# Turning the combined expert rows: from TensorE transposes to an HBM round trip with VectorE block transposes, and a new order of scores and projection

## The reference

```
xn  = layernorm(x)
q, k, v = xn @ w_qkv.T + b_qkv
s   = softmax(q k^T / sqrt(512)) v @ w_out.T + b_out
full_w = softmax of the two largest router logits, zero for the other 6 experts
combined = sum_e full_w[e] * silu(xn @ expert_w[e] + expert_b[e])
y   = xn + combined @ proj_w + proj_b
g   = silu(norm_w * y / rms(y))
out = x + s * g
```

## Time and profile before

| | |
|---|---|
| time, median of 3 runs (lowest to highest) | 490.71 us (489.35 to 492.29) |
| the profiled execution: its own time | 490.71 us |
| its span, first to last instruction | 489.0 us |
| busy: TensorE, VectorE, ScalarE, GpSimd | 98%, 64%, 42%, 42% of the span |
| TensorE's granted clock, mean | 0.999 of 2.4 GHz |

### The profile page before, as it was taken

The page is one execution under the profiler, slowest core; times in us unless marked ns, Lnnn a source line. Parts: engine busy times, 40 slices in busy tenths (PEclk is TensorE's granted clock), DMA queues, the critical chain, the costliest instruction groups (busy, mean ns, idle before and its releaser), DMA issues.

```text
span 489.0 us, 7145 instructions
## 1 busy us (share of the span) xinstructions
PE 478.2 (98%) x2146; PEld 388.1 (79%) x2147; DVE 312.5 (64%) x474; ACT 207.7 (42%) x300; POOL 205.4 (42%) x289
## 2 busy tenths in 40 slices
PE   6999999999999999999999999999999999999995
PEld 3688787888888888878888888878888878888884
DVE  2657152578632436979888888762597754857762
ACT  1265463143331154736444444322655441644550
POOL 2145210005887859703000000744568873377234
PEclk9999999999999999999999999999999999999999
DMA  8764999966888599897996666897555864445512
GB/s 309 272 238 166 379 382 369 390 207 227 294 294 304 188 334 304 252 295 205 262 282 202 195 200 184 310 305 267 158 156 170 264 192 147 138 158 170 172 47 84
DMA packets 77630, 115.77 MB, mean 237 GB/s; under 512 B 6608, under 2 KB 36320, under 8 KB 77600
## 3 DMA queue, kind: packets, MB, share of 16 engines
q1 hardware_dynamic: 63872, 77.62, 50.4%
q0 software_dynamic: 7440, 25.45, 14.7%
q10 hardware_dynamic: 6288, 12.33, 7.1%
HBM read 66.09 MB, written 49.28 MB: 236 GB/s over the span
## 4 chain that ended last, share of the span: by engine, by line
PE 92%; DVE 3%; DMA 2%; issue 2%; SPq 0%; ACT 0%; DVEq 0%
PE ab L1589 20%; PE ab L1590 20%; PE ab L1591 20%; PE sc L1589 7%; PE sc L1591 7%; PE sc L1590 7%; PE sc L1605 3%; PE tp L1595 2%; DMA xg<-rows_scratch 2%; PE tp L1639 2%; DVE y L1468 1%; PE sc L1668 1%; DMA raw_v<-in_w_qkv 1%; PE ab L1613 1%; PE sc L1671 1%
## 5 line engine op out<-in xcount | busy, mean ns | idle before, releaser
L781 POOL DMA_INDIRECT y<-y_scratch,pos x32 | 33.3, 1042 | 88.8 <-DMA y_scratch<-yt_so 74.2
L1589 PE MATMUL ab<-W,st_h 128*128 x156 | 60.8, 390 | 0.6 <-DVE st_l L1297 0.6
L1591 PE MATMUL ab<-W,st_l 128*128 x156 | 60.7, 389 | 0.0
L1590 PE MATMUL ab<-W,st_h 128*128 x156 | 60.7, 389 | 0.0
L764 POOL DMA_INDIRECT rows_scratch<-xb,pos x32 | 31.2, 974 | 51.0 <-DVEq L1285 42.8
L1589 PE MATMUL sc<-xt_h,t_h 128*128 128x512 f32 x128 | 50.1, 391 | 0.0
L1591 PE MATMUL sc<-xt_h,t_l 128*128 128x512 f32 x128 | 49.8, 389 | 0.0
L1590 PE MATMUL sc<-xt_l,t_h 128*128 128x512 f32 x128 | 49.8, 389 | 0.0
L1026 ACT CAST st_h<-tp 128x512 fp32r<-128x512 f32 x39 | 22.9, 587 | 41.1 <-PE ab L1591 39.0
L1353 DVE TENSOR_REDUCE small<-sc 128x1 f32<-128x1024 f32 x16 | 19.5, 1222 | 24.3 <-PE sc L1591 21.9
L1589 PEld LDWEIGHTS ab<-W,st_h 128*128 128x128 f32 x156 | 29.3, 188 | 7.1 <-issue 1.0
(11 more groups left out here) (270 smaller groups left out, 1197.2 us busy)
## 6 DMA issues: line engine op xcount, KB each, us to landing
rows_scratch<-xn ACTq DMA_DIRECT2D x3, 3328.0 KB, 20.2
xb<-in_expert_w POOLq DMA_DIRECT2D x6, 1024.0 KB
xn<-rows_scratch SPq DMA_DIRECT2D x48, 128.0 KB, 3.4
xg<-rows_scratch SPq DMA_DIRECT2D x44, 128.0 KB
y_scratch<-yt_own SPq DMA_DIRECT2D x20, 256.0 KB, 3.1
y_scratch<-yt_so SPq DMA_DIRECT2D x19, 256.0 KB, 2.9
p_scratch<-prob SPq DMA_DIRECT2D x9, 512.0 KB, 2.9
rows_scratch<-xs SPq DMA_DIRECT2D x16, 256.0 KB, 5.9
```

The lines of the kernel that those rows point to most:

```text
L781: pool.indirect_dma_start(y[:, q, :], None, y_d, bass.IndirectOffsetOnAxis(pos[:, GB * s + p:GB * s + p + 1], 0))\
L1589: nc.tensor.matmul(dst, lh, rh, start=start, stop=False)
L1590: nc.tensor.matmul(dst, lh, rl, start=False, stop=False)
L1591: return nc.tensor.matmul(dst, ll, rh, start=False, stop=stop)
```

## The change

The combined rows are no longer transposed by TensorE. ScalarE's queue sends the two tiles of `y1` to HBM (`send_combined`, one transfer), waits for it and fetches them back into `y2` in four transfers of 32 partitions each, in pieces of 128 channels (`fetch_combined`); VectorE turns them with two block transposes (`c_turn`). `y2` is read back in another order of channels, so `add_bias` in the expert stage now writes its rows with the blocks of 32 channels permuted. The semaphore `tp_full` is left to the last probabilities; `p1_turned` counts both kinds of turn by the new table `TURN`, and GpSimd's gathers wait on it. In each step of the loop TensorE does `scores` before `project`. On VectorE `row_max` moves ahead of `add_product`; on ScalarE `exp` moves ahead of `squares`, with a send ahead of `gate` and a fetch behind `exp`. `bc_done` is merged into `pre`.

```diff
+    c_d = nc.dram_tensor("c_scratch", (GB, 2, P, D), F32).ap()
+    c_v = c_d.rearrange("p t s h -> p s t h")
+    c_q = c_d.rearrange("p t (r s) (a f) -> p a s t r f", r=4, a=4)
...
-              + [u for j in range(GB) for u in ([("p", j + 2, 0), ("p", j + 2, 1)] if j + 2 < GB else [])
-                 + ([("t", 1, 1, n) for n in range(KC)] if j == QB - 2 else []) + [("a", 1, j)]]):
+              + [u for j in range(GB) for u in ([("t", 1, 1, n) for n in range(KC)] if j == QB - 2 else [])
+                 + ([("p", j + 2, 0), ("p", j + 2, 1)] if j + 2 < GB else []) + [("a", 1, j)]]):
...
-                    pool.wait_ge(tp_full, j + 3)
+                    pool.wait_ge(p1_turned, TURN["c", j + 2])
...
+            def send_combined(p):
+                act.wait_ge(c_done, 2 * p + 2)
+                act.dma_start(c_v[p], y1[:, 2 * (p % 2):2 * (p % 2) + 2, :]).then_inc(comb_out, 16)
+
+            def fetch_combined(p):
+                act.wait_ge(comb_out, 16 * (p + 1))
+                for a in range(4):
+                    act.dma_start(y2[32 * a:32 * (a + 1), 2 * (p % 2):2 * (p % 2) + 2, :]
+                                  .rearrange("p t (r f) -> p (t r) f", r=4),
+                                  c_q[p, a, :, :, :, :].rearrange("s t r f -> s (t r) f")).then_inc(comb_in, 16)
...
-                vec.tensor_tensor(yt[h], ab[:, (U["e", 0] + h) % 2, :],
-                                  bias_e[:, ds(e, 1), :].rearrange("p a n -> p (a n)"), ALU.add).then_inc(ab_read, 1)
+                vec.tensor_tensor(yt[h].rearrange("p (a c q) -> p c a q", a=4, q=32),
+                                  ab[:, (U["e", 0] + h) % 2, :].rearrange("p (c a q) -> p c a q", a=4, q=32),
+                                  bias_e[:, ds(e, 1), :].rearrange("p o (c a q) -> p (o c) a q", a=4, q=32),
+                                  ALU.add).then_inc(ab_read, 1)
...
+            def c_turn(p):
+                q = 2 * (p % 2)
+                dve.wait_ge(comb_in, 64 * (p + 1))
+                if p == 0:
+                    dve.wait_ge(g_lo, ROWS)
+                else:
+                    dve.wait_ge(tp_lo, TU["c", p])
+                for s in range(2):
+                    last = vec.transpose(tp[:, s, :, :].rearrange("p c (r s) -> p c r s", r=4),
+                                         y2[:, q + s, :].rearrange("p (r c q) -> p c r q", r=4, q=32))
+                last.then_inc(p1_turned, 1)
...
             for j in range(GB):
-                if j + 2 < GB:
-                    project(j + 2)
                 if j == QB - 2:
                     for n in range(KC):
                         key_weights(1, 1, n)
                 if j + 2 < GB:
                     scores(1, j + 2)
-                if j + 3 < GB:
-                    turn_comb(j + 3)
+                    project(j + 2)
```

More of the change, by code:

```diff
@@ L109, in gated_attention_moe @@
         TU[k] = len(TU)
+    TURN = {}
+    for k in ([("c", 0), ("c", 1), ("c", 2), ("t", 0)]
+              + [u for j in range(GB - 2) for u in ([("c", j + 3)] if j + 3 < GB else []) + [("t", j + 1)]]):
+        TURN[k] = len(TURN) + 1
     with ExitStack() as ctx:
@@ L351, in gated_attention_moe @@
         p1_in = sem("p1_in")
+        comb_out = sem("comb_out")
+        comb_in = sem("comb_in")
         p1_turned = sem("p1_turned")
@@ L822, in _ @@
             add_bias_0(1)
-            pool.wait_ge(tp_full, 1)
+            pool.wait_ge(p1_turned, TURN["c", 0])
             gather_pair(2)
@@ L1071, in p_split @@
                 if j < GB - 1:
-                    act.wait_ge(p1_turned, j + 1)
+                    act.wait_ge(p1_turned, TURN["t", j])
                 else:
-                    act.wait_ge(tp_full, GB + 1)
+                    act.wait_ge(tp_full, 1)
                 if 1 <= j != GB - 2:
@@ L1111, in _ @@
                     own_split(SLOT_TILES + t + 2)
+                if t == GB - 2:
+                    send_combined(0)
                 v_hi(1, t)
+            fetch_combined(0)
             act.wait_ge(first_done, 2)
+            t_hi(1, 0, 0)
+            send_combined(1)
+            t_hi(1, 0, 1)
+            t_hi(1, 0, 2)
             c_split(0)
-            for n in range(KC):
-                t_hi(1, 0, n)
+            fetch_combined(1)
+            t_hi(1, 0, 3)
             squares(0)
             c_split(1)
+            send_combined(2)
             exp(0)
             gate(0)
+            fetch_combined(2)
             squares(1)
@@ L1128, in _ @@
                     p_split(GB - 1)
+                if j + 3 < GB:
+                    send_combined(j + 3)
+                if j == QB - 2:
+                    for n in range(KC):
+                        t_hi(1, 1, n)
                 if j + 1 < GB:
@@ L1131, in _ @@
                 if j + 2 < GB:
+                    exp(j + 2)
+                if j + 3 < GB:
+                    fetch_combined(j + 3)
+                if j + 2 < GB:
                     squares(j + 2)
-                if j == QB - 2:
-                    for n in range(KC):
-                        t_hi(1, 1, n)
                 if j + 3 < GB:
@@ L1538, in _ @@
             combine(1)
+            t_lo(1, 0, 0)
+            t_lo(1, 0, 1)
+            c_turn(0)
+            t_lo(1, 0, 2)
             c_low(0)
-            for n in range(KC):
-                t_lo(1, 0, n)
+            t_lo(1, 0, 3)
             dve.wait_ge(vec2_in, 32)
@@ L1544, in _ @@
             add_product(0, 1)
+            c_turn(1)
             c_low(1)
@@ L1550, in _ @@
             add_product(1, 1)
+            c_turn(2)
             c_low(2)
@@ L1560, in _ @@
                     p_low(j)
-                if j + 2 < GB:
-                    add_product(j + 2, 0)
-                    add_product(j + 2, 1)
                 if j == QB - 2:
@@ L1566, in _ @@
                         t_lo(1, 1, n)
+                if j + 2 < GB:
+                    row_max(GB + j + 2)
+                    add_product(j + 2, 0)
+                    add_product(j + 2, 1)
                 if j == GB - 2:
@@ L1574, in _ @@
                     weigh(j + 2)
-                    row_max(GB + j + 2)
+                if j + 3 < GB:
+                    c_turn(j + 3)
                 if j == GB - 3:
```

26 lines of the change are left out of this document (5 added, 21 removed).

## The result

The changed kernel takes 524.43 us (median of 4 runs, 523.3 to 525.28) against 491.45 us for the kernel before on the same chip: ratio 1.0676, interval [1.0632, 1.0721]. The forecast was 494.4 us. The direction was right, and the size was wrong by a factor of nine: +33 us instead of +3.7, far outside the range.

A forecast was written before the change was run, and what follows sets the result against it. TensorE, busy 478.2 of 489.0 us, was taken as the bound. Waits of 11.2 us from a 17.8 us round against a 16.3 us step, less 7.5 gained, put +3.7 on 490.7: 494.4 us, forecast range 493.2 to 499, whole range 488.8 to 499.

The forecast's parts named there:

- The fetch, 4.6 us: Fetch of a combined pair into y2, first issue until landed: 4.6 us, from an earlier round trip of four 128 KB transfers.
- the upper bound of 8.0: Fetch time from above: the fourth issue 1.35 us behind the first plus the largest landing, 6.7, gives 8.0 us.
- The send: ScalarE's send of the combined pair, first link of the added round, priced at 0.45 us.
- The rival "the fetch lands late": Fetch lands at 8.0 us among residuals and probabilities; waits sum to some 29 us, 512 us; chance 0.04.
- The gross gain, 7.5 us: TensorE without eight turns of 0.89 us (7.1) and without a 0.35 us wait for a projection read.
- with all waits hidden: Extreme of the faster rival (chance 0.12): the whole 7.5 us gain is kept, 483.2 us.
- Added at no price: ScalarE's five further issues hidden in idle time, block transposes fitting VectorE's step, gathers some 3 us later at the first.
- Places of the waits: TensorE waits, 11.2 us in all, at project(0), attend_late(0), (1) and (4), two key_weights and the last probabilities.
- the block transposes (1.3 us a pair): VectorE's two block transposes in each pair's round, 1.3 us, fitting into the 16.3 us step.
- `combine` at 2.4 us in the loop: VectorE's combine of the next pair, taken at 2.37 us beside GpSimd's add_x1; lower bound 1.30.
- `add_bias` at 0.69 us: Expert stage: add_bias keeps 32 adjacent channels, so its time was left at 0.69 us.
- an expert stage without new waits: No TensorE wait in the expert stage; rival that permuted writes slow it, up to 8 us, 502, chance 0.04.

The follow-up runs named there:

- e3: Changed kernel with SyncE waiting for the first fetch to land before issuing its early loads (gate rows, residuals, s and x); 522.57 us.
- e14: Changed kernel with small residual, s and x loads in the loop, few gathered rows for pairs 4 to 7 and few probabilities moved; 506.58 us.
- e9: Changed kernel with 34 unread matmuls ahead of project(0), written to a free bank of the scores so they run in the wait; 526.64 us.
- e7: Changed kernel without sends and fetches, c_turn reading y1 directly and leaving out the exchange between partition quarters; 492.32 us.
- e15: Kernel before, in the new order, with each TensorE turn of a combined pair cut from 8 transposes to 2; 491.98 us.
- e10: e8 plus SyncE's early loads behind the first two fetches, gathers ahead of add_x1, and combine, c_turn and send moved earlier in the loop; 509.82 us.
- e6: Kernel before in the new order, TensorE still turning, with ScalarE also sending and fetching every pair into rows nobody reads; 502.81 us.
- e4: Changed kernel with fetches in 2 KB rows instead of 512-byte pieces, leaving out the exchange between partition quarters; 516.98 us.
- e8: Changed kernel with combine, send and fetch of pairs 3 to 7 moved ahead, each round about half a step earlier; 511.92 us.

## Why the prediction was wrong, point by point

- **The fetch, 4.6 us: this step failed.** It took 13.9, 4.8, 11.3, 8.0, 10.9 and 5.0 us for the six pairs for which VectorE waited. I priced it by the earlier trace rows, round trips at a DMA share of 0.69 (103 to 108 us), and even the upper bound of 8.0 was from these rows. Only pairs 2 and 7, the quieter ones, kept the price. e3 and e14 show that it is the company: with it gone the same fetch takes at most 4.4 to 6.1 us.
- **The send** stood in my round as 0.45 us, its issue; its landing was not in the sum. It took 7.3 us for pair 0, and the fetch waited for it. In the loop it was covered: pair 3's fetch went out 3.2 us behind its send, where the forecast had 4.5.
- **The rival "the fetch lands late"** was the right case and had a chance of 0.04. It said 29 us of waits, and 27.9 came. It gave 512 us because it left TensorE's own time unchanged, where 11.2 us of slow matmuls came on top. e9 got 2.4 us of them back, and the time did not fall.
- **The gross gain, 7.5 us: failed too, hidden by the first.** I took TensorE's 98% for a bound that holds alone. e7 and e15 show VectorE's list so near behind it at the key weights of j = 2 that shorter turns become waits there, with a low clock behind them: 491.98 us with a quarter of each turn left. I had priced `times_s` and `weigh` at 0.6 us an instruction; beside GpSimd's additions single ones took 1.7 to 3.6. The forecast of 483.2 us "with all waits hidden" names a case that no run reached: without any transfer it is 492.3, with 6.4 us of waits.
- **Added at no price: partly wrong.** The issues and the wait for the send hold ScalarE's first `t_hi` back, 1.2 us of TensorE's waits; in the loop no such wait is seen. GpSimd's first gather went out 14 us later (340.81 against 326.50), not some 3, but `combine(2)` did not wait for it.
- **Places of the waits.** Forecast against measured: `project(0)` 0.4, 8.0; `attend_late(0)` 2.3, 2.8; `attend_late(1)` 1.7, 3.1; `key_weights(1, 1, 1)` 3.4, 5.1; `key_weights(1, 1, 2)` 2.3, 0.5; `attend_late(4)` 0.5, 0.95; the last probabilities 0.6, 0.7. Not foreseen: 1.2 at `key_weights(1, 0, 2)`, and 2.0 at `project(3)` and 3.7 at `project(6)`, both on a late fetch. The list of places was nearly complete; the sizes were not.
- **Right:** the block transposes (1.3 us a pair), `combine` at 2.4 us in the loop and 1.4 where GpSimd's `add_x1` is absent, `add_bias` at 0.69 us with its new order of channels, an expert stage without new waits (its one wait of TensorE is 1.4 us, 0.6 before).

Of the 33.0 us, then, each run taken over its own kernel before: order and the round without its transfers, 1.8 net (e7, where the gain of the turns is spent at the key weights); the transfers with little beside them in the loop, 14.2 us (e14 less e7), of which 8.0 are the wait of `project(0)` behind SyncE's early loads and 4.0 a wait at `attend_late(0)`, behind pair 2's fetch, whose surroundings e14 left as they were (6.0 us); the crowd in the loop, 17.0 us (the changed kernel less e14).

What stays open: how much of the wait at `attend_late(0)`, 2.8 us in the changed kernel, 1.2 in e3, 4.6 in e10, 4.0 in e14 and none in e7, is the fetch of pair 2 and how much the list behind it, since no run took that one fetch away; and what each added queue costs the probabilities and gathers themselves, which e6 was meant to tell; and what e7 and e15 would take if no instruction of VectorE met GpSimd's.

## What to carry to other kernels

Before a tile is sent through HBM, read the DMA share of the windows in which its transfers would run, not the landing time of like transfers elsewhere: at a share near 1.0 the price was two to three times the quiet one, and moving the other loads away moved the wait to the next fetch. Beside long packets of another queue, long pieces of one's own get a larger share. A round trip on a chain must have its slack before it is added, and the landing of the send counts in it as much as the fetch. And a busy share of 98% does not say that shortening this engine gains: cut its work first in a kernel that does nothing else (as e15), and see whether the time falls.

## What the runs showed of the hardware

- The fetch in 512-byte pieces took 13.9 us and in 2 KB pieces 9.5 us when another queue filled the DMA engines, and 4.8 against 4.7 us when they were not full.
- Two queues with much to move got the same number of packets, not of bytes: 528 of 2 KB against 517 of 0.5 KB (changed kernel, 330 to 334 us), 321 against 317 in e4.
- VectorE's instructions on two 128x512 operands, 0.68 us by themselves, took 2.49 (e15), 3.13 (e7) and 3.60 us (e8) where GpSimd added tiles of that shape at the same time.
- After a wait of 8.0 us the matmuls ran 0.43 us apart with a granted clock of 0.50 from 340 to 345 us; also after the 2.4 us wait of e8 they did so for about 3 us. With unread matmuls in the wait the clock stayed at 1.00 (e9).
- 34 unread matmuls in TensorE's wait kept its clock up and did not shorten the run (+36.5 us over the kernel before against +33.0 without them); the same 34 behind the wait made it +43.5.
